# A linear-attention and mixture-of-experts layer: reciprocal by logarithm and exponential, and four steps moved in the order of three engines

## The reference, cut to what matters

```python
h = _layernorm(x) * (1 + ca) + sa               # x: (16, 512, 128)
q, k = feature_map(split(h @ Wq.T + bq)), feature_map(split(h @ Wk.T + bk))   # 16 heads of 8, 32 features
v = split(h @ Wv.T + bv)
kv, ksum = einsum('nlm,nld->nmd', k, v), sum(k, axis=1)
out = einsum('nlm,nmd->nld', q, [kv | ksum])
out = out[..., :-1] / out[..., -1:]             # the division that is changed
x = x + ga * (out @ Wo.T + bo)
h = _layernorm(x) * (1 + cb) + sb
e = argmax(h @ gate_W + gate_b)                 # one of 8 experts for each token
x = x + gb * (gelu(h @ W1[e] + b1[e]) @ W2[e] + b2[e])
```

## Time and profile before

| | |
|---|---|
| median of 3 runs | 429.49 us (427.32 to 431.19) |
| the profiled execution | 431.88 us |
| its span, first to last instruction | 430.0 us |
| busy: PE, DVE, ACT, POOL | 373.3, 300.8, 272.9, 201.6 us |
| first denominators' product to the last batch's (L1060) | 27.5 to 256.3 us |
| block phase, by the last batch's end | about 258 to 420 us |

### The profile page before, as it was taken

How to read it: one execution, slowest core, us unless ns; L and a number is a source line. 1 busy time by engine, 2 the same in 40 slices (tenths; PEclk the granted TensorE clock), 3 DMA queues, 4 the chain that set the end, 5 groups by cost and what they waited for, 6 DMA issues and landing times.

```text
span 430.0 us, 12990 instructions
## 1 busy us (share of the span) xinstructions
PE 373.3 (87%) x4487; PEld 284.5 (66%) x4487; DVE 300.8 (70%) x1106; ACT 272.9 (63%) x710; POOL 201.6 (47%) x226
## 2 busy tenths in 40 slices
PE   3598959999999999999999977998787899999990
PEld 1354636565655565565556537987787799999990
DVE  3536858987988898879867878777365566665651
ACT  2676754787687669667776726654554376657660
POOL 1210334553843664565546425455546354554452
PEclk9999998999999999999999989999898899999996
DMA  6458962112211221221122147344434455554410
GB/s 199 158 188 320 374 187 101 58 45 101 79 63 64 96 81 40 88 99 57 49 101 76 57 134 224 96 108 141 149 113 146 140 187 182 147 147 121 123 32 2
DMA packets 30782, 52.38 MB, mean 122 GB/s; under 512 B 4194, under 2 KB 22758, under 8 KB 30336
## 3 DMA queue, kind: packets, MB, share of 16 engines
q1 hardware_dynamic: 24352, 34.50, 26.5%
q0 software_dynamic: 6368, 17.05, 10.9%
HBM read 28.46 MB, written 19.34 MB: 111 GB/s over the span
## 4 chain that ended last, share of the span: by engine, by line
PE 55%; ACT 17%; DVE 13%; issue 7%; another core or an unknown queue 3%; DVEq 2%; DMA 1%; POOL 1%; POOLq 0%; SPq 0%; ACTq 0%
PE ps_proj L1188 10%; PE ps_feat L1175 6%; PE ps_proj L1028 4%; PE ps_proj L995 4%; DVE rden L720 4%; PE ps_out L1076 3%; PE ps_den L1060 3%; PE ps_proj L1031 3%; ACT kf L531 3%; PE ps_kv L1175 3%; PE ps_feat L1016 3%; PE ps_den L1175 3%; ACT qf L536 3%; ACT shared L516 2%
## 5 line engine op out<-in xcount | busy, mean ns | idle before, releaser
L473 POOL DMA_INDIRECT out<-kf,modb x71 | 70.6, 995 | 75.2 <-DVE kf L926 67.3
L1188 PE MATMUL ps_proj<-w2sb,qf 128*128 x568 | 77.1, 281 | 0.0
L440 POOL DMA_INDIRECT experts_lists<-pay,slot x64 | 63.5, 992 | 17.6 <-issue 17.6
L1188 PEld LDWEIGHTS ps_proj<-w2sb,qf 128*128 128x128 f32 x568 | 71.3, 197 | 0.0
L586 ACT ACTIVATE xT<-ps_out 128x128 f32<-128x128 f32 x71 | 19.7, 278 | 62.5 <-PE ps_out L1168 45.0
L720 DVE RECIPROCAL rden<-den 128x512 f32<-128x512 f32 x16 | 53.6, 3351 | 5.6 <-ACT den L570 5.3
L921 DVE TENSOR_TENSOR kf<-ps_proj,firsts_sb 128x128 f32<-128x128 f32 x71 | 20.7, 291 | 51.0 <-PE ps_proj L1188 22.9
L536 ACT ACTIVATE qf<-ps_proj 128x512 f32<-128x512 f32 x32 | 17.4, 595 | 45.8 <-PE ps_feat L1031 45.8
L427 POOL TENSOR_TENSOR wo<-wsb,modb 128x128 f32<-128x128 f32 x16 | 7.5, 469 | 82.3 <-ACT den L570 82.3
L1175 PE MATMUL ps_feat<-xT,shared 128*128 128x128 f32 x288 | 39.6, 281 | 5.4 <-ACT xT L586 3.6
L594 ACT ACTIVATE qf<-ps_feat,shared 128x128 f32<-128x128 f32 x144 | 41.0, 376 | 0.0
(11 more groups left out here) (177 smaller groups left out, 965.1 us busy)
## 6 DMA issues: line engine op xcount, KB each, us to landing
modb<-experts_lists SPq DMA_DIRECT2D x71, 196.0 KB
xall<-in_x SPq DMA_DIRECT2D x16, 256.0 KB, 2.9
pay<-modb SPq DMA_DIRECT2D x16, 256.0 KB, 2.6
modb<-modulation_rows SPq DMA_DIRECT2D x1, 3072.0 KB, 11.0
firsts_sb<-in_firsts SPq DMA_DIRECT2D x1, 2576.0 KB, 16.9
experts_lists<-padding SPq DMA_DIRECT2D x9, 196.0 KB
out<-kf,modb POOLq DMA_INDIRECT x71
modb<-modulation_rows SPq DMA_DIRECT2D x1, 1024.0 KB, 5.1
```

What stands on the lines that cost most here:

```text
L440: g_.indirect_dma_start(out=lists, in_=pay[b.home][:, t, :], in_offset=None, out_offset=bass.IndirectOffsetOnAxis(ap=slot[b.home][:, t:t + ...
L473: g_.indirect_dma_start(out=rows_out, in_=yb[u], in_offset=None, out_offset=bass.IndirectOffsetOnAxis(ap=token, axis=0), bounds_check=last ...
L1188: ins = mm(Y[u % 2][:, 0:D], g[u % R4][:, c * P:(c + 1) * P], w2sb[:, bass.ds(e * DFF + c * D, D)], start=(c == 0), stop=(c == FC - 1))
```

## The change

Five things are changed.

1. The denominators' eviction on ACT is a logarithm (Ln) instead of an identity, and ACT then takes the exponential of its negative, which is a first value of the reciprocal. DVE improves it by a Newton step of two instructions, the first of which writes into PSUM bank `G`. The result has the opposite sign, so the residual subtracts. The table set with both functions is loaded at the start.
2. ACT's batch: `h2T_copy` stands between the first two k features; `normalise1(b+1)` stands after the k features of batch b (before: `normalise1(b+2)` at the end of batch b); `kvm_copy` stands between k values and k squares.
3. POOL's batch: `rstd1_of` stands at the end of even batch b, behind `gated` and `scatter` (before: at its beginning).
4. Last batch: on PE `count(0)` stands behind `v_project`, `table_transpose(0)` behind `q_features` and the ranks behind `attend`; on DVE `slots` stands behind the first four copies of expert weights.
5. Waits for `s_denp` that guard bank `G` become waits for the Newton step's `s_rdst`.

```diff
@@ POOL, batch
-                if ahead and b.par == 0:
-                    rstd1_of(b.half + 3, b=b + 2)
                 if not first:
                     rstd2_of(b + -1, rows_of=None if second else b + -2)
                 gated(b, first)
                 if not first and not second:
                     scatter(b + -2)
+                if ahead and b.par == 0:
+                    rstd1_of(b.half + 3, b=b + 2)
@@ ACT
+            a.preload_act_table_set("natural_log_exp_and_others")
...
                 k_feature(b, 0)
-                k_feature(b, 1)
                 if not first and not second:
                     h2T_copy(b + -2)
+                k_feature(b, 1)
                 v_values(b)
...
                 k_feature(b, 3)
+                if not first and not last:
+                    normalise1(b + 1)
                 q_feature(b, 0)
...
                 if not last:
-                    k_parts(b + 1)
-                act.wait_ge(s_kvt, b.v + 1)
-                a.activation(kvm[:], G[:, 0:2 * P], ACT.Copy).then_inc(s_kvm, 1)
+                    k_values(b + 1)
+                kvm_copy(b)
                 if not last:
+                    k_squares(b + 1)
                     q_parts(b + 1)
                 act.wait_ge(s_den, b.v + 1)
                 act.wait_ge(s_eps, b.v + 1)
-                a.activation(den[:], G[:], ACT.Identity, bias=kveps[:, 1:2]).then_inc(s_denp, 1)
-                if b.v + 2 < B:
-                    normalise1(b + 2)
+                a.activation(den[:], G[:], ACT.Ln, bias=kveps[:, 1:2]).then_inc(s_denp, 1)
+                act.wait_ge(s_denp, b.v + 1)
+                a.activation(rden[:], den[:], ACT.Exp, scale=-1.0).then_inc(s_rden, 1)
@@ DVE
             def attention(b):
-                dve.wait_ge(s_denp, b.v + 1)
-                v.reciprocal(rden[:], den[:]).then_inc(s_rden, 1)
                 dve.wait_ge(s_rden, b.v + 1)
+                v.scalar_tensor_tensor(out=G[:], in0=G[:], scalar=kveps[:, 1:2], in1=rden[:],
+                                       op0=ALU.add, op1=ALU.mult).then_inc(s_rdst, 1)
+                dve.wait_ge(s_rdst, 2 * b.v + 1)
+                v.scalar_tensor_tensor(out=rden[:], in0=G[:], scalar=2.0, in1=rden[:],
+                                       op0=ALU.subtract, op1=ALU.mult).then_inc(s_rdst, 1)
+                dve.wait_ge(s_rdst, 2 * b.v + 2)
...
@@ DVE, batch
                 if last:
                     table_rows(0)
-                if not first and not second:
+                    kv_values(b)
                     experts(b + -2)
-                kv_values(b, first)
-                if not first and not second:
-                    slots(b + -2)
+                elif not first and not second:
+                    experts(b + -2)
+                if not last:
+                    kv_values(b, first)
+                    if not first and not second:
+                        slots(b + -2)
...
                     for k in range(R4):
                         copy_firsts(k)
+                    slots(b + -2)
                 attention(b)
@@ PE, batch
-                if last:
-                    count(0)
                 k_features(b, first)
                 if not first and not second:
                     transpose_h2(b + -2, first=third)
                 v_project(b)
+                if last:
+                    count(0)
                 if not first and not second:
                     gate(b + -2)
                 if not first:
                     out_project(b + -1)
-                if last:
-                    table_transpose(0)
                 if not first and not second:
                     gate_transpose(b + -2)
                 q_features(b)
                 if not last:
                     transpose_xn(b + 1, first)
+                else:
+                    table_transpose(0)
                 kv_product(b, first)
                 if not last:
                     project(b + 1, 0)
-                if not first and not second:
+                if not first and not second and not last:
                     rank(b + -2, first=third)
                 kv_transpose(b)
                 if not last:
                     project(b + 1, 1)
                 attend(b)
+                if last:
+                    rank(b + -2)
```

More of the change, by code:

```diff
@@ L270, in build @@
         s_denp = sem("den_ready")
-        s_rden = sem("rden_ready")
+        s_rden = sem("rden_first_value_ready")
+        s_rdst = sem("rden_step")
         s_oT = sem("oT_ready")
@@ L510, in modulate, with k_values @@
                     .then_inc(s_hT, 1)
-            def k_parts(b):
+            def k_values(b):
                 act.wait_ge(s_proj, 3 * b.v + 1)
@@ L516, in k_parts, with k_squares, kvm_copy @@
                 a.activation(kvals, PJ[0][:, :], ACT.Identity, bias=bias).then_inc(s_kst, 1)
+            def k_squares(b):
+                bias = wsb[:, W_BIAS:W_BIAS + 1]
                 a.activation(ksqs, PJ[0][:, :], ACT.Square, bias=bias).then_inc(s_kst, 1)
+            def kvm_copy(b):
+                act.wait_ge(s_kvt, b.v + 1)
+                a.activation(kvm[:], G[:, 0:2 * P], ACT.Copy).then_inc(s_kvm, 1)
             def q_parts(b):
@@ L577, in _ @@
             modulate(start)
-            k_parts(start)
+            k_values(start)
+            k_squares(start)
             q_parts(start)
@@ L730, in residual @@
                     dve.wait_ge(s_scat[b.home], scattered(b.v - HOMES))
-                v.tensor_tensor(pay[b.home][:, :, X2:X2 + D], bank[:, :].rearrange("p (t d) -> p t d", t=LT),
-                                xall[:, b.v * LT:(b.v + 1) * LT, :], ALU.add).then_inc(s_x2, 1)
+                v.tensor_tensor(pay[b.home][:, :, X2:X2 + D], xall[:, b.v * LT:(b.v + 1) * LT, :],
+                                bank[:, :].rearrange("p (t d) -> p t d", t=LT), ALU.subtract).then_inc(s_x2, 1)
             def second_stats(b):
@@ L1115, in count @@
                 if part == 0:
-                    pe.wait_ge(s_denp, B - 1)
+                    pe.wait_ge(s_rdst, 2 * (B - 1))
                 mm(counts[part], ones_bf[:], seen[:], start=True, stop=True).then_inc(s_cnt, 1)
@@ L1198, in _ @@
                 if k == 2:
-                    pe.wait_ge(s_denp, B)
+                    pe.wait_ge(s_rdst, 2 * B)
                 if k == 3:
```

## The result

| | before | after |
|---|---|---|
| median | 430.34 us (427.32 to 431.27, 4 runs) | 452.82 us (451.11 to 457.40, 4 runs) |
| ratio | | 1.055, interval 1.046 to 1.065 |
| profiled execution, its span | 431.88, 430.0 us | 452.81, 451.0 us |
| busy: PE, DVE, ACT, POOL | 373.3, 300.8, 272.9, 201.6 us | 380.5, 270.0, 280.7, 202.0 us |
| from batch 4's product to batch 14's | 148.1 us | 170.7 us |

A forecast was written before the change was run, and what follows sets the result against it. The prediction took PE, with ACT between its parts, to bound the kernel. Its terms, 0.4+16.5-2.4+7.5-3.4 = +18.6 us, put on the median of 429.49, gave 448.0 us; own range 443 to 455, with rival A 438 to 455.

The forecast's parts named there:

- ACT waits for POOL's shift, five batches: Batches 5, 7, 9, 11, 13: ACT's `normalise1` waits 4.2 us for POOL's shift, periods 18.1, +3.3 each, +16.5 us.
- clock behind the wait: PE, idle 3.8 us in those five batches, then runs at half clock: 1.5 each, +7.5 us, bounds 0 and 11.
- even batches 6 to 14: `kvm` ahead of k squares brings the next denominators' product 0.48 sooner: 5 x 0.48, -2.4 us, perhaps half that.
- batch 4's product: Early batches: +1.3 less 0.5 from the late shift, earlier gains lost in a DMA wait: +0.4 us by batch 4.
- last batch: Batch 15's new order: table ready sooner, DVE ends the batch, `oT` ends 22.0 after batch 14's product: -3.4, bounds -1 and -4.5.
- Rival A: Rival: the same wait on ACT and PE, but PE's clock stays up: 440.5 us, chance 0.20.
- The reciprocal: Steady batches: `oT` comes about 1.1 us sooner, but v's copy releases the output projection, so the gain is nothing.
- POOL's products run beside them: `gated`'s products on POOL beside DVE's Newton instructions: nothing to +0.3 us a batch, taken as nothing.
- `h2T` between the k features: ACT's batch: same instructions, same sum before v's copy, so the move is worth nothing.
- Rival C: Rival: ACT's tables are switched between Ln and Exp, 1.28 a load, two per batch: about 458 us, chance 0.05.
- rival D: Rival: little changes, ACT's wait is half of that reckoned and the clock stays up: about 431 us, chance 0.06.
- rival B: Rival: no wait on POOL, each batch gains 0.48 and the last 3.4: 418.9 us, chance 0.07; needs shift by 7.6.

The follow-up runs named there:

- a5: The changed kernel with 15 thrown-away f32 products of 128x128 on PE in its wait, batches 5 to 13 odd: 442.31 us, 1.037 of the kernel before.
- a6: The changed kernel as it is, run again beside others on the same chip: 448.82 us, 1.053 of the kernel before.
- a1: The changed kernel with POOL's scale and shift put back at the beginning of its even batch: 418.86 us, 0.981 of the kernel before.
- e3: The kernel before with only the scale at the end of POOL's even batch and `normalise1(b+1)` behind ACT's k features: 455.61 us, 1.072.
- d1: The changed kernel with the scale first again, and `bog` and the sum into `xall` ahead of `wo` on POOL: 492.12 us, 1.153 of the kernel before.
- e1: The changed kernel with the scale first again, and `bog` alone ahead of POOL's wait for the denominators: 423.25 us, 0.996 of the kernel before.
- b2: The kernel before with only `kvm` moved between k values and k squares on ACT: 420.79 us, 0.987 of the kernel before.
- b1: The kernel before with only the reciprocal changed (Ln, Exp, Newton step, PE's waits on `s_rdst`): 431.61 us, 1.012 of the kernel before.
- e2: The changed kernel with the scale first again and the old reciprocal (identity eviction, no Newton step): 422.50 us, 0.996 of the kernel before.
- c3: The kernel before with only the last batch's new order on PE and DVE: 425.33 us, 1.001 of the kernel before.

## Why the prediction was right, and where it was off

The forecast was 448.0 (438 to 455), the result 452.82, and the mechanism the one named: the wait and the clock, the two large terms, came out within 1 us, and no large errors cancel. Against the profiled spans (+21.0 us):

| step | forecast | measured | from |
|---|---|---|---|
| ACT waits for POOL's shift, five batches | 5 x 3.3 = 16.5 | 5 x 3.2 = 16 | a5: 18.0 less 14.8 |
| clock behind the wait | 5 x 1.5 = 7.5 | 5 x 1.6 = 8 | a6 less a5 |
| even batches 6 to 14 | -2.4 | -1.4 | 4 x 0.20 and 0.62 |
| batch 4's product | +0.4 | +1.9 | 93.54 less 91.63 |
| last batch | -3.4 | -3.55 | `oT` less batch 14's product |
| sum | +18.6 | +21.0 | |

**The wait.** ACT's 4.30 and PE's 3.84 were forecast as 4.2 and 3.8, since POOL's order after the denominators is fixed: products, four indirect DMAs, scale, shift. a1 shows the cause by taking it away, e3 by giving it alone.

**The clock.** One gap of 3.8 us in the trace of before was enough to forecast five. Rival A (clock kept) is out by a5. That all five stretches were of 3.4 us and lay on work was not certain: one in e3 was twice as long.

**The even batches** were mis-sized: 0.20 instead of 0.48. The prediction gave the reason as one it could not exclude: the q exponentials start 0.83 after their products' end while POOL issues DMAs. POOL now runs later against the product (first DMA at 4.67 instead of 4.35), and the posts move with it: the first comes 10.50 after the product instead of 10.13. That the DMAs hold the posts is what d1 and e1 speak for, not a proof. Even b2, where `kvm` stands alone, gains only 0.3 to 0.4 of the 0.48. Batch 14 has the full gain and more; there the first post is on time.

**Batch 4's product.** Its +0.4 takes the gain of 0.48 off twice, for batches 3 and 4, where the text names it once. The shift's wait in batch 3 is there (ACT 2.55, PE 1.81). Most of the 1.5 above the forecast is the execution's: in batch 3 both wait for rows by DMA, and the rows came 1.34 later. POOL's first instruction behind them, before and after:

```profile
60.58 1.01 POOL L419 TENSOR_TENSOR rstd<-ve,mhalf 128x4 f32<-128x4 f32 x1 [8.99 <-DMA pay<-modb]
```
```profile
61.92 1.02 POOL L420 TENSOR_TENSOR rstd<-ve,mhalf 128x4 f32<-128x4 f32 x1 [12.80 <-DMA pay<-modb]
```

Counted from there, batch 4's product comes at 31.05 before and at 31.62 after (31.52 in a6): +0.5 to +0.6 is the change's. The first product was 3.5 us later (31.06 against 27.53; PE was at the low clock until 21.8 instead of 9.8, and the first k projections took 3.78 instead of 1.98), but that is lost in the same wait.

**The reciprocal.** Nothing in the steady batches of the kernel before: b1 confirms it. But the prediction took this over to the changed kernel without asking what the moved `kvm` does to it, and there it does not hold: with the old reciprocal `oT` would end last (b2, e2), and the new one saves 0.24 in every odd batch of a1. The forecast is not touched by it, as it had the new reciprocal in place. Exp took 0.63 (0.60), Newton's instructions 0.75 and 0.69, no longer than `oT`'s 0.75 before, though POOL's products run beside them: no cost from that. The Trainium skill ("GPSIMD Engine Reference", section "8. Key points") names contention with VectorE only for two SBUF inputs or a 2-port mode, and these instructions have one input in PSUM; the trace agrees. The prediction put the last batch's gain on the table and DVE together; c3 and e2 show that half of it or more is the reciprocal's. What it did not see is that the reciprocal alone makes the last batch 5 us longer and `oT` in it 3 us later (b1), because it holds `G` longer.

**`h2T` between the k features** was not run by itself; b2 without it and e2 with it have the same periods. That it is worth nothing, as forecast, holds unless the other moves in e2 hide it.

**The medians.** 452.82 less 430.34 are 22.5 and the spans differ by 21.0; the rest is the executions' spread.

Rival C is out (one load of Ln's and Exp's tables, at 0.72), rival D too. By a1, rival B was near on what the rest of the change is worth (0.981, it had 0.975) and wrong on the condition.

The best version that was run is a1, 0.981: the change with the scale left where it was.

## What to carry to other kernels

Before an engine's step is moved later, list who reads its result and what is queued behind the reader: here 2 us of work on an engine with half its time idle stopped ACT and PE for 4 us in every second batch. Price a new stall on PE with the clock behind it, here 1.6 us on top of 3.2. Two gains that meet at one wait are not a sum: the shorter reciprocal paid only once `kvm` had moved. And when a change has five parts, the whole hides them: POOL's scale cost 7%, the rest was worth -2%.

## What was not expected of the hardware

- While POOL issued four indirect DMAs (5 us), some of PE's semaphore posts came 0.4 to 3.3 us late: the q features' at 2.35 to 3.1 after their start instead of 1.99, the gate's 1.1 late in e1, the k features' 3.3 late in d1. Moving the DMAs by 0.5 us cost 0.6 us per batch, by 1.8 us 6 us per batch.
- An f32 product of 128x128 on PE is two instructions of 0.12 us (28 products, 56 instructions, 6.52 us).
- Behind idle stretches of PE of 3.5 to 4.0 us the granted clock was low for 3.4 us (the changed kernel, all five; e3, four) or 6.8 us (e3 once, d1 in every steady period but one); fillers of 3.6 us in the gap kept it at 1.00. In the last batch it was low behind shorter waits too: 3.4 us behind one of 1.40 (before), 10.2 us behind one of 2.22 (b1).
